# A decoder layer in one pipelined loop: the value bias folded into the output bias, its eviction on ScalarE, weight loads on SyncE, and a new order of the work

## The reference

```python
q = split(x @ Wq.T + bq); k = split(x @ Wk.T + bk); v = split(x @ Wv.T + bv)
q_phi = _apply_kernel(q, orf); k_phi = _apply_kernel(k, orf)   # (exp(proj - norm) + 1e-6) / 8
kv   = einsum('bhlm,bhld->bhmd', k_phi, v);  ksum = sum(k_phi, axis=2)
num  = einsum('bhlm,bhmd->bhld', q_phi, kv); den = einsum('bhlm,bhm->bhl', q_phi, ksum)
out  = (num / den) @ Wo.T + bo
x = layernorm(x + out)
x = layernorm(x + xattn(ctx, x, ctx))
# scale = 1 / mean|w|;  wq = clip(round(w * scale), -1, 1) / scale   for the three FFN weights
x = layernorm(x + bitlinear(silu(bitlinear(x, gate)) * bitlinear(x, up), down))
```

## Time and profile before

| what | value |
|---|---|
| median of 3 runs | 508.16 us (504.93 to 509.95) |
| the profiled execution's own time | 505.92 us |
| its span, first to last instruction | 504.2 us |
| busy: TensorE, VectorE, ScalarE, GpSimd | 438.9, 450.6, 428.8, 365.5 us |
| mean granted TensorE clock | 0.967 |

### The profile page before, as it was taken

One profiled execution on the slowest core, in us unless ns is written; L12 is line 12 of the kernel. 1 busy time (PEld: TensorE's weight loads), 2 busy tenths in 40 slices (PEclk: granted clock), 3 DMA queues, 4 the chain that ended last, 5 costly groups with the idle time before them and its releaser, 6 DMA issues.

```text
span 504.2 us, 18524 instructions
## 1 busy us (share of the span) xinstructions
PE 438.9 (87%) x6566; PEld 304.7 (60%) x6566; DVE 450.6 (89%) x1355; ACT 428.8 (85%) x908; POOL 365.5 (72%) x789
## 2 busy tenths in 40 slices
PE   4568888998999998999999999999999999876641
PEld 2235666666776766776767676777676766543310
DVE  4667686999999999899999999999999999999771
ACT  2247789999999998999999999999999999867532
POOL 1447767778788888788888888888888876763422
PEclk9979899999999999999999999999999999999875
DMA  7665566787768787566666666666666687542212
GB/s 186 230 125 101 133 116 109 107 154 124 127 130 134 157 140 133 133 146 146 146 146 141 140 139 135 144 140 142 136 145 136 137 139 127 85 75 62 55 33 63
DMA packets 192659, 64.27 MB, mean 127 GB/s; under 512 B 172384, under 2 KB 192352, under 8 KB 192608
## 3 DMA queue, kind: packets, MB, share of 16 engines
q1 hardware_dynamic: 190080, 60.46, 60.4%
q10 hardware_dynamic: 2528, 3.15, 1.7%
HBM read 17.31 MB, written 4.19 MB: 43 GB/s over the span
## 4 chain that ended last, share of the span: by engine, by line
PE 58%; ACT 13%; DMA 11%; DVE 7%; issue 5%; SPq 3%; POOL 3%; ACTq 0%; POOLq 0%; DVEq 0%
PE bank L1131 10%; PE bank L1335 9%; DMA tT<-pkT 4%; PE bank L1306 4%; PE bank L1225 4%; PE bank L1362 4%; PE bank L1183 3%; DMA ffn_ld<-in_L_ffn_w_down_dram 3%; PE bank L1204 2%; PE bank L1145 2%; PE bank L1240 2%; PE bank L1322 2%; PE bank L1150 2%; PE bank L1211 2%; PE bank L1294 2%
## 5 line engine op out<-in xcount | busy, mean ns | idle before, releaser
L1131 PE MATMUL bank<-wq_hi,xT 128*128 128x512 f16 (+1 forms) x256 | 72.5, 338 | 3.7 <-DVE vv L816 2.3
L434 POOL TENSOR_TENSOR ve<-mv,lneps 128x1 f32<-128x1 f32 x96 | 19.4, 202 | 63.4 <-DVE mv L866 48.0
L438 POOL TENSOR_TENSOR rs<-ve,mhalf 128x1 f32<-128x1 f32 x96 | 55.0, 573 | 0.0
L946 DVE SCALAR_TENSOR_TENSOR g<-th,bank 128x512 f32<-128x512 f32 x64 | 43.4, 678 | 4.7 <-ACT th L653 4.3
L558 ACT ACTIVATE x<-y,nmr,rs 128x256 f32<-128x256 f32 x64 | 39.8, 622 | 7.9 <-DVE y L1007 4.4
L630 ACT ACTIVATE pT<-bank 128x512 f32<-128x512 f32 x64 | 37.8, 591 | 9.7 <-PE bank L1296 8.1
L897 DVE TENSOR_REDUCE negm<-bank 128x4 f16<-128x512 f32 x64 | 43.4, 678 | 1.6 <-PE bank L1260 1.2
L898 DVE TENSOR_REDUCE negm<-bank 128x4 f16<-128x512 f32 x64 | 43.5, 680 | 0.0
L577 ACT ACTIVATE phk<-bank 128x512 f32<-128x512 f32 x64 | 39.4, 617 | 4.5 <-PE bank L1150 4.5
L1131 PE MATMUL bank<-wq_lo,xT 128*128 128x256 f16 (+1 forms) x128 | 43.2, 337 | 0.0
L425 POOL TENSOR_TENSOR pkA<-qk,pkA 128x512 f16<-128x512 f32 x32 | 37.6, 1175 | 7.0 <-ACT pkA L520 6.6
(11 more groups left out here) (184 smaller groups left out, 1580.0 us busy)
## 6 DMA issues: line engine op xcount, KB each, us to landing
xs<-in_x_dram SPq DMA_DIRECT2D x32, 128.0 KB, 2.3
cs<-in_ctx_dram SPq DMA_DIRECT2D x32, 128.0 KB, 2.3
xr<-in_x_dram SPq DMA_DIRECT2D x32, 128.0 KB, 2.3
out_dram<-ot SPq DMA_DIRECT2D x32, 128.0 KB, 1.8
ffn_ld<-in_L_ffn_w_gate_dram ACTq DMA_DIRECT2D x1, 1024.0 KB, 9.0
ffn_ld<-in_L_ffn_w_up_dram ACTq DMA_DIRECT2D x1, 1024.0 KB, 11.5
ffn_ld<-in_L_ffn_w_down_dram ACTq DMA_DIRECT2D x1, 1024.0 KB, 13.8
pkAT<-pkA SPq DMA_TRANSPOSE x64, 3.2
```

What stands on the lines that cost most here:

```text
L438: g.tensor_tensor(rs[n - 1][:, :], ve[n - 1][:, :], mhalf[:, :], ALU.pow).then_inc(done[f"pw{n}"], 1)
L946: v.scalar_tensor_tensor(g1[:, n, :], th[:, n, :], 1.0, gate, ALU.add, ALU.mult).then_inc(done[f"gl{n}"], 1)
L1131: last = T.matmul(o, xT[:, 2 * part + c, :], w[:, c, cols], start=(n == 0), stop=(n == 5))
```

## The change

1. The value bias leaves the loop. `v_` becomes a ScalarE copy with the same scale. Once, `bv` is loaded as two columns, spread on VectorE, multiplied by `woT` on TensorE (`value_bias`), and added to `bo` on VectorE (`output_bias`) into `bob`.
2. The first two tiles of x, and all weights, are loaded by SyncE in this order: x0, Wq, Wk, Wv, x1, gate, up, bq, bk, bv, down, Wo, bo. ScalarE issues only the four small loads at its start. GpSimd's early wait for `bo` is gone.
3. VectorE does all three magnitudes, the scales and `scaled(0)` ahead of iteration 0, and TensorE transposes Wo and does `ffn_means` ahead of its iteration 0; the remaining rounds, clips, transposes and evictions of the feed-forward weights are done in iterations 0 to 3 (VectorE) and 2 to 6 (TensorE, ScalarE).
4. Each engine has its own number of unrolled iterations ahead of and behind the loop: behind and ahead 13, 14 for SyncE, 11, 12 for GpSimd, 11, 14 for ScalarE, 9, 10 for VectorE and TensorE.
5. The five orders, the lags and nearly all banks are new, and with the banks the waits that guard them. Some waits are left out, others are added (`s1` now has a semaphore of its own, `vh` waits for none).

```diff
-                for n, b in enumerate((bq, bk, bv)):
-                    sp.dma_start(bqkv[:, n * D:(n + 1) * D],
+                for n, b in enumerate((bq, bk)):
+                    sp.dma_start(bqk[:, n * D:(n + 1) * D],
                                  b.rearrange("(a n) -> a n", a=1).to_broadcast([P, D])).then_inc(b_in, 16)
+                with nc.allow_non_contiguous_dma(reason="256 values of a bias, once"):
+                    sp.dma_start(bv_ld[:, :], bv.rearrange("(c p) -> p c", p=P)).then_inc(b_in, 16)
...
-            def v_(t, par):
-                first_time(dve, t, 0, b_in, 48)
-                wait(dve, "vm", t)
-                v.scalar_tensor_tensor(vv[:, par, :, 0:DK], at_v.rearrange("p (h d) -> p h d", h=H), 1.0 / WSCALE,
-                                       bqkv[:, 2 * D:3 * D].rearrange("p (h d) -> p h d", h=H),
-                                       ALU.mult, ALU.add).then_inc(done["v"], 1)
+            def v_(t, par):
+                first_time(act, t, 0, prep, 14)
+                wait(act, "vm", t)
+                copy(vv[:, par, :, 0:DK], at_v.rearrange("p (h d) -> p h d", h=H), "v", 1.0 / WSCALE)
...
+            def output_bias():
+                dve.wait_ge(prep_ps, 6)
+                dve.wait_ge(bo_in, 16)
+                v.tensor_tensor(bob[:, :], at_bias, bo_ld[:, :], ALU.add).then_inc(rep, 1)
...
             feature_weights()
             magnitudes[0]()
+            magnitudes[1]()
+            magnitudes[2]()
+            spread_value_bias()
+            ffn_scales()
+            scales_of[0]()
...
+            def value_bias():
+                pe.wait_ge(prep_ev, 4)
+                pe.wait_ge(rep, 7)
+                for k in range(2):
+                    last = T.matmul(at_bias, bv_rep[:, k, :], woT[:, k, :], start=(k == 0), stop=(k == 1))
+                last.then_inc(prep_ps, 1)
...
             output_weight()
+            ffn_means()
```

More of the change, by code:

```diff
@@ L281, in first_time, with run @@
                 eng.wait_ge(semaphore, v)
-        def run(eng, iteration, lags=LAGS, first=FIRST):
+        def run(eng, iteration, lags, first):
             for i in range(first):
@@ L561, in x1_ @@
             def x1_(t, par):
+                wait(act, "rs1", t)
                 wait(act, "ya2", t, -2)
@@ L707, in _ @@
+            run(act, iteration, 11, 14)
         @block.vector
@@ L1060, in iteration @@
                 go(y2, i, par, 6)
-                once(clear_values, i, 4)
-                go(gl1, i, par, 7)
-                go(hu0, i, par, 7)
                 go(hu1, i, par, 7)
-                go(tlo, i, par, 4)
-            run(dve, iteration)
+                once(rounds_of[2], i, 3)
+                go(hh0, i, par, 7)
+                once(clips_of[0], i, 0)
+                once(clips_of[2], i, 3)
+                go(ad3, i, par, 8)
+                go(hh1, i, par, 7)
+                once(scales_of[2], i, 2)
@@ L1069, in _ @@
+                go(tlo, i, par, 4)
+                go(ad1, i, par, 3)
+                once(scales_of[1], i, 1)
+                go(hx, i, par, 7)
+                go(am, i, par, 6)
+                go(hc, i, par, 7)
+                go(ac, i, par, 6)
+                go(hr, i, par, 7)
+                go(ar, i, par, 6)
+            run(dve, iteration, 9, 10)
         @block.tensor
@@ new lines, in iteration @@
+                go(ntp, i, par, 4)
+                go(xqTp, i, par, 8)
+                go(kvs, i, par, 3)
+                go(pv1, i, par, 7)
+                go(s0, i, par, 6)
+                go(pv0, i, par, 7)
+                if isinstance(i, int) and i == 6:
+                    pe.wait_ge(done["nT"], 3)
+                once(ternaries[5], i, 6)
+                go(s1, i, par, 6)
+                if isinstance(i, int) and i == 2:
+                    pe.wait_ge(done["xT"], 2)
+                once(ternaries[0], i, 2)
@@ new lines, in iteration @@
+                go(phq0, i, par, 3)
+                go(g0, i, par, 8)
+                go(oxp, i, par, 7)
+                once(ternaries[1], i, 2)
+                go(g1_, i, par, 8)
+                go(vm, i, par, 1)
+                go(xTp, i, par, 0)
+                if isinstance(i, int) and i == 4:
+                    pe.wait_ge(ffn_out, 3)
+                once(ternaries[3], i, 4)
+                if isinstance(i, int) and i == 3:
+                    pe.wait_ge(rep, 8)
+                once(ternaries[2], i, 3)
@@ L1414, in iteration @@
-                go(vhp, i, par, 5)
-            run(pe, iteration)
+            run(pe, iteration, 9, 10)
 _INS = ["x", "ctx_1024", "L0_attn_Wq", "L0_attn_bq", "L0_attn_Wk", "L0_attn_bk", "L0_attn_Wv", "L0_attn_bv",
```

414 lines of the change are left out of this document (193 added, 221 removed), and 6 rows, old and new, of the table done.

## The result

The changed kernel takes 530.97 us (median of 6 runs, 529.49 to 533.18), the kernel before 507.70 on the same chip (6 runs). The ratio is 1.0467, 95% interval [1.0433, 1.0501]: slower by 4.7%, where 503.0 was forecast. The profiled execution took 531.87 us with a span of 530.1, against 504.2, so 25.9 us have to be found.

A forecast was written before the change was run, and what follows sets the result against it. TensorE was taken to set 13.0 us a tile in the loop. Fill -2.7, loop entry -2, orders 0 and emptying 0 sum to -4.7, taken from 508.2 and rounded to 503.0 us, range 492 to 515.

The forecast's parts named there:

- Part 5: New engine orders in the loop: 0 us a tile, bounds -0.1 and +0.35; pipeline depth and mode changes the same.
- two other rules: Trainium skill: a second load issuer only saves issue time (start); a change of tiling mode drains TensorE (orders).
- Part 1: Value bias, loop: VectorE loses 0.33 us a tile, ScalarE gains 0.26; zero taken, cost at most 6, gain at most 7.6.
- rival A: Loop slower: ScalarE becomes as full as TensorE, 0.35 us a tile more, 514.5 us; chance 0.20.
- Part 2: Start: sums and means come first, so tile 0's q and k eviction falls at 25.7 us, 7.1 later.
- Part 3: Fill: +7.1 for the start, -7.3 and -2.5 recovered, -2.7 us in all, bounds +7 and -8.
- Part 4: Loop entry: unrolled tiles 8 to 15 gain from each engine's own entry, -2 us, bounds 0 and -3.5.
- Part 6: Emptying after tile 31: the last tile's chain keeps its steps and sequence, 0 us, bounds -3 and +3.
- B: Rival, no change: the start's 7 us are not recovered in the fill, +2.4 or 510.5 us; chance 0.17.
- C: Rival, much faster: VectorE's fixed order held the loop, relief of 0.3 a tile gives 7 more, 496 us; chance 0.13.

The follow-up runs named there:

- Experiment 4: Changed kernel, every order as it is, with GpSimd's `lo` cut from 128x512 to 128x8: 517.99 us, ratio 1.0176.
- experiment 5: Kernel before, every order as it is, with one 128x512 GpSimd product added beside `xm`: 535.63 us, ratio 1.0564.
- experiments 1 and 2: Changed kernel, first with GpSimd's second-norm chain ahead of the third's: 528.57 us; second with `xm` written by `scalar_tensor_tensor`: 533.59 us.
- experiment 7's first kernel: Kernel before with only the value bias moved into the output bias and `v` evicted by ScalarE: 515.42 us, ratio 1.0187.
- experiment 11: Kernel before with own loop entries and the changed kernel's load order: 509.28 us; with Wo right behind the three projections, bo awaited by the residual alone: 502.15.
- Experiment 9: Changed kernel with sums 2 and 3, spread bias and scales behind tile 0's eviction, Wo's preparation an iteration later: 526.59 us; with GpSimd's order also rearranged: 518.05.
- experiment 10: Kernel before with nothing but own loop entries for each engine: 505.22 us; changed kernel with the common loop entry of before: 529.80 us.
- edit 3: Changed kernel with GpSimd's order rearranged, so that `lo` runs while `x2` is made and 128x1 operations run beside `xm`: 521.34 us, ratio 1.0246.
- Experiment 7: `v`'s ScalarE eviction cut to one head of sixteen: 529.52 us in the changed kernel, 517.69 with GpSimd's order rearranged and the start undone.

## Why the prediction was wrong, point by point

**Part 5, the orders, is the step that failed.** I took 0 a tile with a bound of +0.35; it was +0.81 in the loop, from 13.01 to 13.82. I compared TensorE's list, its mode switches and the depth of the pipeline, and took each duration on VectorE as a constant of the instruction. Neither GpSimd's order nor what would run beside what entered the sum. Experiment 4 takes one GpSimd operation away, with every order as it is, and 13.8 of the 14.9 us of tiles 8 to 31 go; experiment 5 puts one in and `xm` grows in the old order. From `xm`'s start to the next start on VectorE it is 0.70 us more (0.26 before, 0.87 and 1.05 in turn after), 16 us over 23 tiles, of which 13.8 are seen. What runs in place of TensorE's own pace is a round: VectorE's `ox`, GpSimd's order from `y` to the end of `lo`, the end of `xm` 0.15 us behind it, and VectorE's order back to `ox`. Its pieces add up to the interval in the changed kernel and in experiments 1 and 2.

The Trainium skill ("SBUF — State Buffer", Who interferes with whom) states this as a rule: a VectorE instruction in a two-port mode, which `tensor_scalar` from SBUF to SBUF can enter, or one with two SBUF inputs while GpSimd's reads SBUF, contends with GpSimd for a shared pair of ports, and whoever comes second is blocked until the other's instruction is done. The trace agrees for large operations, with `xm` ending 0.15 us behind `lo` as `tensor_scalar` and 0.28 with two inputs. It does not bear the rule out for the small ones: in the kernel before `xm` starts 0.12 us into a 128x1 `pow` recorded at 0.56 and takes its usual 0.345; whether the `pow` holds the ports for only part of its recorded length no run shows. The prediction weighed two other rules and not this one; a list of VectorE's SBUF-to-SBUF operations against their new GpSimd neighbours would have shown `xm` beside `lo`.

**Part 1, the value bias: mechanism half right, cover misjudged.** The bound of 6 us was the answer for the old order: experiment 7's first kernel takes 6.3 more over tiles 8 to 31, 0.27 a tile. That is all of the 0.26, so the 0.2 that I read as slack on ScalarE covered none of it; rival A had this wait right. In the changed kernel it costs nothing, since the round is longer still. The 0.33 that VectorE lost was more than spent by the 0.70 on `xm`.

**Part 2, the start, was right:** tile 0 at 26.5, 25.7 forecast. The sums and means stood on its way as worked out; VectorE waited 0.96 us for the down weight, since it came to it earlier than I had counted:

```profile
13.20 4.47 DVE L801 TENSOR_REDUCE wsum<-ffn_ld 128x1 f32<-128x2048 f32 x2
18.63 2.29 DVE L801 TENSOR_REDUCE wsum<-ffn_ld 128x1 f32<-128x2048 f32 x1 [0.96 <-DMA ffn_ld<-in_L_ffn_w_down_dram]
...
26.48 0.69 DVE L841 SCALAR_TENSOR_TENSOR qk<-bank,bqk 128x512 f32<-128x512 f32 x1 [2.84 <-PE bank L1162]
```

`value_bias` took 2.0, at my upper end. One thing I missed: TensorE waited 11.5 us for Wo, until 19.4. It was hidden only because the means came at 20.97; experiment 11 shows it bare: tile 0 at 26.3, 7.7 later than before.

**Part 3, the fill, was wrong in size.** -2.7 forecast, +6.0 measured, close to my bound of +7. The stretch from tile 0 to 7 did shrink, from 69.1 to 67.2, by 1.9 where I had counted 9.8. Experiment 9 splits it: undoing the start moves tile 8 by 2.4 only, so most of the late start was indeed recovered by tile 8. But then tile 8 is still at 104.0, though tile 0 came 2.1 earlier than before. The other 3.6 are left, by elimination, to the new orders in the fill and the earlier feed-forward preparation: loads and entries alone, with Wo moved up, bring tile 8 to 97.5 (experiment 11), and without the collision it comes no earlier (107.1 in experiment 4). In the fill GpSimd is held up too, beside the large feed-forward operations that now run from iteration 0: `xb` took 1.76 where the loop has 0.73. Timelines of GpSimd and VectorE:

```profile
41.67 1.76 POOL L438 TENSOR_TENSOR xb<-xr,bob 128x256 f32<-128x256 f32 x1
```

```profile
41.56 1.28 DVE L820 TENSOR_SCALAR ffn_t<-ffn_ld,wscale 128x2048 f32<-128x2048 f32 x1
```

How much of the 3.6 this is was not measured.

**Part 4, loop entries:** -2 forecast. In the old order tiles 8 to 16 gain 1.7 us as forecast, but the ratio of 0.9976 is 1.2 us, with an interval that just touches no change, and the steady interval is 13.08 for 13.01; in the new order no gain is seen.

**Part 6, the emptying:** 0 forecast with bounds of 3, +5.0 measured. It stays at 105 to 106 with `lo` cut, with GpSimd's order changed and with the start undone. In the old orders it is 100.7 to 102.3 in three runs (`v` on ScalarE, and the two of experiment 11), but 105.0 in the kernel before with nothing but own entries (experiment 10). With one profiled execution of each, it can't be put down to the orders; the cause stays open.

**The rivals.** A had the right sign and the wrong engine: it named ScalarE and priced 0.35 a tile. B (the start not recovered) does not hold for the changed kernel, where experiment 9 leaves 2.4 of 10 us, but it is seen beside edit 3 (6.1 of 9.8) and in the old orders, where tile 0's 7.7 us of experiment 11 are still 4.3 at tile 8. C fell. What is left open: the versions without the collision stand at 13.17 to 13.22 a tile, about 0.2 over the kernel before. Some 0.07 of that is also in the old orders with own entries (13.07 to 13.08 in experiments 10 and 11). Experiment 7 shows that the rest is not ScalarE's `v`; the chains run through the transposes' DMA and TensorE in turn, and I have no run that names one.

## What to carry to other kernels

An instruction's duration is not its own when another engine can hold its port: before a reordering, list the SBUF-to-SBUF operations of VectorE and the large operations of GpSimd, and see which pairs will meet. When three engines are busy for 94 to 97% and the pace has still fallen, compare the durations of single instructions before and after: the grouped rows with min/median/max show a stretched one. If its end lies at a fixed distance behind another engine's instruction, its length is a wait, and the round that sets the pace runs through that engine, although the chain of waits books the time on the held one. And test parts of a bundle alone: here the whole loses 4.7%, while its loads and entries alone, with Wo moved up to where TensorE's order needs it, gain 1.1%.

## What the hardware showed that I had not expected

`xm` (128x256 float32, SBUF to SBUF) ends 0.146 to 0.154 us behind GpSimd's 128x512 operation, in the changed kernel and in experiments 1 and 5. Undisturbed its recorded length is 0.345 us, so less than a whole execution follows the release. With two SBUF inputs it is 0.28 behind. A GpSimd `pow` on 128x1, recorded at 0.56 us, did not lengthen it at all. And the norm's statistics, 128x256 read from SBUF, kept their 0.42 us beside a GpSimd subtraction of the same size.
